# Contraction index of two einsums in another order: DVE turns contiguous runs, loads by quarters of 32 partitions, the first weight group turned by DVE

## What is computed

```python
def reference(x, itok_B_0_15, itok_B_3_7, L0_cond_weights, L1_cond_weight):
    W = L0_cond_weights[itok_B_0_15]            # (128, 64, 64)
    x = x + jnp.einsum('bct,bcd->bdt', x, W)
    w = L1_cond_weight[itok_B_3_7]              # (128, 1024, 1024), from (8, 1024, 1024)
    return x + jnp.einsum('bsi,boi->bso', x, w)
```

## Time and profile before

| | |
|---|---|
| runs, us | 842.97, 842.06, 842.00 (median 842.06) |
| the profiled execution | 842.41, its span 840.7 |
| TensorE matmul busy | 809.3 us (96%), mean granted clock 0.992 |
| VectorE, ScalarE, GpSimd busy | 450.0 (54%), 277.4 (33%), 28.4 (3%) |
| transfers | 90.84 MB, mean 108 GB/s, 34.9% of the 16 engines' span |

### The profile page before, as it was taken

One profiled execution on the slowest core, in us unless ns is written; L12 is line 12 of the kernel. 1 busy time (PEld: TensorE's weight loads), 2 busy tenths in 40 slices (PEclk: granted clock), 3 DMA queues, 4 the chain that ended last, 5 costly groups with the idle time before them and its releaser, 6 DMA issues.

```text
span 840.7 us, 17121 instructions
## 1 busy us (share of the span) xinstructions
PE 809.3 (96%) x3572; PEld 667.7 (79%) x3573; DVE 450.0 (54%) x466; ACT 277.4 (33%) x515; POOL 28.4 (3%) x61
## 2 busy tenths in 40 slices
PE   3599999999999999999999999999999999999997
PEld 2588888788887888888888888888888888888885
DVE  5556665565666544565654466656443443344342
ACT  2333332423243333233333324333332322332232
POOL 3100000000000000000000000000000000000000
PEclk9799999999999999999999999999999999999999
DMA  4433433333433423333434334333332223223222
GB/s 140 148 112 107 126 108 125 114 115 107 126 118 117 129 80 100 115 114 121 129 101 126 105 105 128 110 126 117 114 91 83 83 87 87 88 75 96 85 83 85
DMA packets 66655, 90.84 MB, mean 108 GB/s; under 512 B 6228, under 2 KB 57428, under 8 KB 66644
## 3 DMA queue, kind: packets, MB, share of 16 engines
q1 hardware_dynamic: 66644, 90.72, 34.9%
HBM read 57.15 MB, written 33.55 MB: 108 GB/s over the span
## 4 chain that ended last, share of the span: by engine, by line
PE 69%; SPq 19%; issue 5%; DMA 3%; DVE 2%; ACT 1%; ACTq 0%; DVEq 0%; POOL 0%; POOLq 0%
PE z_ps L454 10%; PE z_ps L455 10%; PE first_ps L455 10%; PE first_ps L454 10%; PE z_ps L457 10%; PE first_ps L457 9%; SPq L343 5%; SPq L192 5%; SPq L360 4%; PE y_ps L468 3%; PE y_ps L469 3%; PE y_ps L470 3%; SPq L374 2%; DMA w_nat<-in_L_cond_weight_dram 1%; DMA y<-in_L_cond_weight_dram 1%
## 5 line engine op out<-in xcount | busy, mean ns | idle before, releaser
L454 PE MATMUL z_ps<-w_hi,xt_hi 128*128 (+1 forms) x528 | 205.6, 389 | 0.7 <-DVE xt_lo L725 0.7
L454 PE MATMUL first_ps<-w_hi,xt_hi 128*128 x528 | 205.4, 389 | 0.0
L455 PE MATMUL z_ps<-w_lo,xt_hi 128*128 (+1 forms) x528 | 205.4, 389 | 0.0
L455 PE MATMUL first_ps<-w_lo,xt_hi 128*128 x528 | 205.4, 389 | 0.0
L457 PE MATMUL z_ps<-w_hi,xt_lo 128*128 (+1 forms) x512 | 199.2, 389 | 0.0
L457 PE MATMUL first_ps<-w_hi,xt_lo 128*128 x480 | 186.7, 389 | 0.0
L716 DVE STREAM_TRANSPOSE x_turned<-x_in 128x1024 f32<-128x1024 f32 x67 | 143.5, 2142 | 34.5 <-issue 17.3
L548 ACT ACTIVATE xt_hi<-x_turned 128x1024 fp32r<-128x1024 f32 x67 | 71.0, 1060 | 237.5 <-DVE x_turned L716 237.5
L454 PEld LDWEIGHTS z_ps<-w_hi,xt_hi 128*128 128x128 f32 x528 | 99.1, 188 | 22.0 <-issue 1.1
L454 PEld LDWEIGHTS first_ps<-w_hi,xt_hi 128*128 128x128 f32 x528 | 99.1, 188 | 20.8
L455 PEld LDWEIGHTS first_ps<-w_lo,xt_hi 128*128 128x128 f32 x528 | 99.1, 188 | 20.6
(11 more groups left out here) (119 smaller groups left out, 414.9 us busy)
## 6 DMA issues: line engine op xcount, KB each, us to landing
x_in<-in_x_dram SPq DMA_DIRECT2D x272, 128.0 KB
out_dram<-y SPq DMA_DIRECT2D x128, 256.0 KB, 3.4
w_nat<-in_L_cond_weight_dram SPq DMA_DIRECT2D x128, 128.0 KB
w_nat<-in_L_cond_weight_dram SPq DMA_DIRECT2D x4, 512.0 KB, 6.6
w_turned<-in_L_cond_weight_dram SPq DMA_DIRECT2D x2, 512.0 KB, 3.9
y<-in_L_cond_weight_dram SPq DMA_DIRECT2D x2, 512.0 KB, 8.0
x_turned<-in_L_cond_weights_dram SPq DMA_DIRECT2D x2, 256.0 KB, 3.9
ids_i<-in_itok_B_dram SPq DMA_DIRECT2D x2, 0.5 KB, 2.1
```

The costliest lines, as they stand in the source:

```text
L454: nc.tensor.matmul(to, xt_hi[h][:, t, :], whi, start=(t == 0), stop=False)
L455: mm = nc.tensor.matmul(to, xt_hi[h][:, t, :], wlo, start=False, stop=last and not pair)
```

## The change

Contracted column is now 256 a + 32 t + m: tile t takes runs of 32 columns, and the transposition reads its input in runs (`"p (b t m) -> p b t m"`), for x and for the weights alike. All loads of x and of weights go one quarter a at a time, 32 partitions outermost on both sides: x in 8 transfers of 64 KB instead of 4 of 128 KB, a chunk in 4 of 128 KB as before. The first group uses the same layout and loads (4 transfers a chunk instead of one), is turned by VectorE into `w_turned`, and its chunks hold rows of every quarter of the outputs. It has five places to load to, one of them x_in[1]. Chunks 1, 3, 5 and 7 are issued by ScalarE. TensorE's transpositions and their PSUM banks go.

```diff
-    x_blocks = x.rearrange("n (b r) (a m) -> n b a r m", a=BLOCKS, r=BLOCK)
+    x_quarters = x.rearrange("n (b r) (a m) -> n a r b m", a=BLOCKS, r=BLOCK)
-    adapter_rows = adapter_w.rearrange("n o i -> (n o) i")
-    adapter_blocks = adapter_w.rearrange("n (b k r) (a m) -> n k b a r m", a=BLOCKS, b=BLOCKS, r=BLOCK)
+    adapter_quarters = adapter_w.rearrange("n (b k r) (a m) -> n k a r b m", a=BLOCKS, b=BLOCKS, r=BLOCK)
-        first_nat = [w_nat[:, 0], w_nat[:, 1], w_turned[:, 0], w_turned[:, 1], y[0][:], y[1][:], w_nat[:, 0], w_nat[:, 1]]
-        OWN_PLACE = 6
+        first_places = [w_nat[:, 0], w_nat[:, 1], y[0][:], y[1][:], x_in[1][:]]
+        OWN_PLACE = len(first_places)
+        first_nat = [first_places[c % OWN_PLACE] for c in range(CHUNKS_PER_GROUP)]
-        PER_X = BLOCKS * 16
+        PER_X = 2 * BLOCKS * 16
+        def in_quarter(to, a):
+            return to[a * BLOCK:(a + 1) * BLOCK].rearrange("r (b m) -> r b m", m=QUARTER)
...
             def load_first(c):
                 if c >= OWN_PLACE:
-                    sp.wait_ge(first_turned, NH * (c - OWN_PLACE) + NH)
-                sp.dma_start(first_nat[c], adapter_rows[bass.ds((first_ad * CHUNKS_PER_GROUP + c) * P, P), :]
-                             ).then_inc(first_loaded[c], 16)
-            for c in range(2):
-                load_first(c)
+                    sp.wait_ge(first_turned, c - OWN_PLACE + 1)
+                for a in range(BLOCKS):
+                    sp.dma_start(in_quarter(first_nat[c], a),
+                                 adapter_quarters[bass.ds(first_ad, 1), c, a].rearrange("n r b m -> (n r) b m")
+                                 ).then_inc(first_loaded[c], 16)
+            load_first(0)
             sp.wait_ge(table_made, 1)
             sp.dma_start(slot_row[:, 1:LOOKED_UP + 1, :], table_i[0:LOOKED_UP]).then_inc(table_moved, 16)
-            for c in range(2, 5):
-                load_first(c)
+            load_first(2)
             sp.wait_ge(table_ready, 1)
...
-                for first_block, sample in zip((0, BLOCKS // 2), samples):
-                    for b in range(BLOCKS // 2):
-                        at = (first_block + b) * QUARTER
-                        sp.dma_start(x_in[h][:, at:at + QUARTER],
-                                     x_blocks[bass.ds(sample, 1), b].rearrange("n a r m -> (n a) r m")
+                if places_free is not None:
+                    sp.wait_ge(first_turned, places_free)
+                for half, sample in enumerate(samples):
+                    for a in range(BLOCKS):
+                        sp.dma_start(in_quarter(x_in[h][:, half * HALF:(half + 1) * HALF], a),
+                                     x_quarters[bass.ds(sample, 1), a].rearrange("n r b m -> (n r) b m")
                                      ).then_inc(x_loaded[h], 16)
...
-                            for b in range(BLOCKS):
-                                sp.dma_start(w_nat[:, q, b * QUARTER:(b + 1) * QUARTER],
-                                             blocks[:, :, b].rearrange("n k a r m -> (n k a) r m")
+                            for a in range(BLOCKS):
+                                sp.dma_start(in_quarter(w_nat[:, q], a),
+                                             quarters[:, :, a].rearrange("n k r b m -> (n k r) b m")
...
+            load_first(4)
             load_x(0, 0)
-            for c in range(5, CHUNKS_PER_GROUP):
-                load_first(c)
-            load_x(1, 1)
-            sp.wait_ge(first_turned, NH * CHUNKS_PER_GROUP)
+            load_first(6)
+            load_x(1, 1, places_free=OWN_PLACE)
+            sp.wait_ge(first_turned, CHUNKS_PER_GROUP)
...
-            for c in range(CHUNKS_PER_GROUP):
-                turn_first(c)
...
-                pe.wait_ge(first_lo_made, NH * TPB)
+                pe.wait_ge(first_lo_made, CHUNKS_PER_GROUP)
...
+            act.wait_ge(groups_ready, 1)
+            first_ad = act.value_load(group_row[0:1, 0:1], min_val=0, max_val=NAD - 1)
+            load_first(1)
+            load_first(3)
             act.wait_ge(w0_with_1, 1)
             nc.scalar.activation(w0_all[:, 0], w0_nat, ACT.Copy).then_inc(w0_hi_made, 1)
...
+            keep_first_hi(0)
+            load_first(5)
+            for c in range(1, 3):
+                keep_first_hi(c)
+            load_first(7)
...
+            def turn_first(c):
+                dve.wait_ge(first_with_1, c + 1)
+                if c >= 2:
+                    dve.wait_ge(first_lo_made, c - 1)
+                nc.vector.transpose(w_turned[:, c % 2].rearrange("p (t b m) -> p b t m", b=BLOCKS, m=BLOCK),
+                                    first_nat[c].rearrange("p (b t m) -> p b t m", b=BLOCKS, m=BLOCK)
+                                    ).then_inc(first_turned, 1)
...
-                                w_nat[:, q].rearrange("p (b m t) -> p b t m", b=BLOCKS, m=BLOCK)
+                                w_nat[:, q].rearrange("p (b t m) -> p b t m", b=BLOCKS, m=BLOCK)
...
-                                    x_in[h][:].rearrange("p (b m t) -> p b t m", b=BLOCKS, m=BLOCK)
+                                    x_in[h][:].rearrange("p (b t m) -> p b t m", b=BLOCKS, m=BLOCK)
...
-            for c in range(4):
-                keep_first_lo(c)
+            turn_first(0)
+            for c in range(1, 5):
+                turn_first(c)
+                keep_first_lo(c - 1)
             dve.wait_ge(w0_zeroed, 1)
             dve.wait_ge(table_ready, 1)
             turn_x(0, 0)
+            keep_first_lo(4)
             keep_xt_lo(0, 0)
-            for c in range(4, CHUNKS_PER_GROUP):
+            for c in range(5, CHUNKS_PER_GROUP):
+                turn_first(c)
                 keep_first_lo(c)
```

More of the change, by code:

```diff
@@ L133, in conditional_residual_kernel @@
         y_ps = [bank(f"y_ps{n}") for n in range(NH)]
-        first_banks = [[bank(f"first_ps{k}{n}") for n in range(NH)] for k in range(2)] + [y_ps]
-        z_banks = [z_ps, first_banks[0]]
-        TURNS = len(first_banks)
+        odd_ps = [bank(f"odd_ps{n}") for n in range(NH)]
+        z_banks = [z_ps, odd_ps]
         ranks_ps, counts_ps = z_ps[0][:, 0:NAD], z_ps[1][:, 0:NAD]
@@ L760, in _ @@
             turn_x(0, 0)
+            keep_first_lo(4)
             keep_xt_lo(0, 0)
-            for c in range(4, CHUNKS_PER_GROUP):
+            for c in range(5, CHUNKS_PER_GROUP):
+                turn_first(c)
                 keep_first_lo(c)
-            dve.wait_ge(first_lo_made, NH * CHUNKS_PER_GROUP)
+            dve.wait_ge(first_lo_made, CHUNKS_PER_GROUP)
             dve.sem_inc(chunk_lo_made, CHUNKS_PER_GROUP)
```

50 lines of the change are left out of this document (23 added, 27 removed).

## The result

| | before | after |
|---|---|---|
| median of the runs, us | 842.51 (842.0 to 842.97) | **850.13** (849.47 to 850.86) |
| ratio | 1 | **1.0088**, 95% interval 1.0073 to 1.0103 |
| span of the profiled execution, us | 840.7 | 847.8 |
| first z matmul, us | 36.72 | 46.48 |
| first y matmul, pass 1 / pass 65, us | 53.16 / 826.55 | 64.67 / 833.60 |

Slower by 7.6 us, where 16.5 were forecast. The page after: the span, TensorE, the chain that ended last, the two turns' and the subtraction's groups (busy us, mean ns | idle before), and the median us from issue to landing of a chunk.

The account below looks back on a forecast made before the run. TensorE was taken as the bound, though not alone: SP's queue falls behind in trains. Span 840.7 + 8.7 (start) + 2.0 (clock) + 5.8 (passes) = 857.2, plus 1.4 around it: 858.6 us; own range 852 to 866, 8-in-10 range 847 to 872.

Parts of the forecast that it names:

- The turn: VectorE's transposition of 1024 elements, reading runs instead of every eighth element: 1.2 us instead of 2.13.
- the rival that it stays at 2.13: Turns unchanged: start 8 us longer, chunk path 0.9 longer, three trains losing about 1 us each; 870 us, chance 0.13.
- The turn is worth nothing directly in the passes: In the passes, DVE is off TensorE's path except behind a late chunk, so faster turns gain nothing directly.
- allowed lag: How far SP's x issue may trail TensorE's pass before TensorE waits: 9.1 us before, 12.6 after.
- The start: Before the first z matmul: DVE's chain of nine turns and nine subtractions puts it at 45.4 us, 8.7 later.
- The transfers do not set it: At the start: new loads use 16 engines, 4.7 MB at 393 GB/s in 12 us, so landings do not delay z.
- The clock: First z matmuls: nothing runs on TensorE before, so some 4.1 us at half speed, costing 2.0 us.
- The queue: SP's issues in the passes: x in 8 transfers costs +1.3 us, a chunk -0.8; TensorE's waits net +5.8 us.
- A pass of a train becomes 13.8: SP's pace in the eight passes loading the next group's weights: 13.30 us plus 0.5.
- the lag account: Over the passes: adds up how far SP's queue trails TensorE; trains two to four exceed the allowed 12.6 us.
- TensorE waits 10.4: In trains two to four, TensorE waits 10.4 us in all, against 4.6 measured before.
- the queue keeps up: SP's queue in trains: transfers at 0.30 or gaps under 0.17 us remove the old 4.6 us waits; 848.2 us, chance 0.14.

Follow-up runs that it names:

- The table of waits: Kernels with old or new loads, start and turns; waits, step/runs: old loads 25.5/17.3 us (old start), 17.9/11.0 (new); new loads 3.0/0, 3.2/0.
- the one with work up to z: Changed kernel with asserted bounds plus idle TensorE transpositions, 16 after the sixth chunk's w_lo and 24 after the seventh's: 848.61 us.
- both with bounds: Kernel before with looked-up numbers that waits depend on asserted: 862.49 us; the same plus new loads, x and later chunks turned in runs: 834.68 us.

## Why the prediction was right or wrong

**The turn**: right. 1.25 us for an estimate of 1.2; the rival that it stays at 2.13 is out, and with the step put back into the kernel after, and nothing else changed, it is 2.14 again. The Trainium skill's page SBUF — State Buffer (section Door 1) says that each access that crosses to a new 16-byte line pays a penalty, and with a step of 32 bytes every element does; the two lengths agree with it.

**The turn is worth nothing directly in the passes**: wrong. The table of waits says 3 us with new loads, 7 to 8 with old ones. I took only the chunk's turn into the path (0.9 us of allowed lag); x's turn stands ahead of it on the same engine, which would make it 1.8 for each train's end (that fits the 7 to 8, but no run takes the two turns apart). And with new loads the step puts VectorE's serial pass over TensorE's, a limit that I did not look for. The rival's 3 us in the passes came out (3.2 measured), but by this limit and not by the queue: luck.

**The start**: the number nearly right (46.48 for 45.4), a reason wrong. "The transfers do not set it" took 393 GB/s from loads by rows for loads by quarters. They moved 234 at a DMA share of 1.10. Chunks 0 and 1 landed at 18.2, the table's transfer, issued at 14.37 behind them, at 20.1, and SP issues x only after it; VectorE stood 3.7 us waiting for landings. By rows it was 2.5 us shorter. The Trainium skill, page SBUF — State Buffer, section Door 1, says that 32 partitions reach 8 of SBUF's 16 ports, gives 189 GB/s for 1 MiB into them and 328 into all 128. I left that rule out. The rates here have the same order, 211 GB/s for rows of 4 KB in 32 partitions and 328 for the same in 128, but they don't test it: the 211 come from transfers into all four quarters in turn, not far under the 260 that their issues allow. VectorE's own work was 2.6 us shorter than counted (it was free at 17.65 instead of 18.2, and its chain took 25.2 without the landings instead of 27.2), so most of the error was hidden in the sum, by luck: 45.4 - 2.6 + 3.7 = 46.5.

**The clock**: right, 1.75 for 2.0, and shown apart: 1.3 to 2.5 in the seven kernels in which TensorE does nothing for 33 us or more ahead of z, and all gone in the one with work up to z.

**The queue**: this is the step that failed. "A pass of a train becomes 13.8"; it became 12.28 (12.21 in the pass shown). Of the 1.6 us between 13.8 and that pass, x is 0.47 (8 issues in 3.83 us for 4.3: 0.317 each for 0.34, and 0.18 between two for 0.23), the chunk 0.16 (1.84 for 2.0), and 0.98 I had not thought of: the stretches between the transfers, which hold table looks of SP, became shorter. The looks' median went from 0.86 to 0.67 us, in every kernel with the new loads and in no other; why isn't shown. So the lag account ran on a wrong pace, the lag stayed at 2.1 us where 12.6 were allowed, and "TensorE waits 10.4" is 0. Its form was right: the measured lags pass 9.1 where the kernel before waits.

The rival "the queue keeps up" came true in its outcome. Neither of its two conditions did (a transfer cost 0.317 and not 0.30, the gap was 0.18 and not under 0.17); the two misses together are what it wanted, since at these prices x and the chunk bring a pass from 13.30 to 13.15 even with the looks as before. Its time of 848.2 is 1.9 under the measured 850.1: the first z matmul came 1.1 later than forecast, the clock took 0.25 less, and 2.3 us instead of 1.4 lie around the span, as the profiled execution was the fastest of the four.

**The sum**, term by term: first z +9.8 for +8.7; clock +1.75 for +2.0; passes -4.5 for +5.8; around the span 2.3 for 1.4. The passes alone are off by 10.3, and the others hide 1.8 of it: 858.6 - 10.3 + 1.8 = 850.1. The chance of 0.14 for that rival was too small: no row measured the price that my pace went by, and 0.5 us a pass decided 10.

**What was expected to pay and where it went**: the loads and turns are worth 27.8 us (862.49 to 834.68, both with bounds); the start by VectorE takes 15.1 of them back. Without the asserted bounds the kernel before stands at 842.5, so there loads and turns are worth 7.8 or a little more (834.7 still carries the bounds), and the new start costs about twice that. No version without the bounds and with the loads alone was run.

## What to carry to other kernels

Take a change apart before it is judged: here one part (the form of the loads) is faster, another (the first group on VectorE) is slower by more, and together they looked like a loss. A queue that is slower than the bound engine in some stretches costs nothing up to an allowance and then its whole excess; find out how far it is from that edge by adding half a microsecond a pass. And put table looks where an engine waits anyway: in a serial pass they are on the path as much as a turn. Last, look at the clock behind a wait: short waits of TensorE can bring a stretch at half speed with them, which no view of waits shows.

## What the runs showed of the hardware

- A few instructions of 0.02 us and longer looks, 0.6 to 0.7 us in a pass of SP, made 20 us at the end of one kernel and nothing in the other. Of the 20, 4.7 were three stretches of 3.4 us in which the clock was granted at 0.50, behind waits of TensorE of 1.9 to 2.0 us.
- SP's look at the table, a load of a few numbers, took 0.67 us in the median with the new loads and 0.86 with the old ones.
- An issue costs 0.32 to 0.38 us for 32 or 128 matching partitions, 0.55 for 64 matching ones and for 128 from a 4 x 32 source.
- Transfers into 32 partitions each, one quarter after the other, moved 211 to 234 GB/s with the DMA engines busy at a share of 0.7 to 1.1; 128 partitions with 4 KB each 328 at 0.87, with 1 KB each 226 at 0.74; the old form 88 at a share of 0.26.
- TensorE at the 1.2 GHz level shows in the spacing of its matmuls, 0.43 against 0.23 us. Where a trace has no record of the clock yet, as ahead of 50.2 us after the change, a view prints 1.00 all the same. TensorE work that ended 4.9 us ahead of z left z at 0.50 for 6 us; ended 0.76 us ahead, z ran at full speed.
